# A routed attention and an FP4 feed-forward block on one core: weights decoded by pairs of units, the first LayerNorm folded, three gate/up banks, a staggered start

## The chip, the cores and the metric

The kernel runs on one core of a Trainium2 chip. The metric is the device time of one execution in microseconds (us). Engines: TensorE (PE; its weight loads are PEld), VectorE (DVE), ScalarE (ACT), GpSimd (POOL) and SyncE (SP), whose queue issues most DMAs. Each engine executes its own instructions in order and waits on semaphores for the others.

## The reference, cut to what matters

```
x = x + tanh(g_xattn) * attention(layernorm(x), ctx, router, W_q, b_q, token_sets)
x = x + tanh(g_ffn)   * ffn(layernorm(x), gate, up, down)     # weights: FP4 codes and block scales

attention: scores = ((x W_q^T + b_q) router^T) / sqrt(256), masked to a token's 4 drawn sets;
           softmax over the 2 largest, times ctx (64 sets x 256) of that sequence
ffn:       gate = x Wg^T, up = x Wu^T, out = (gelu_tanh(gate) * up) Wd^T, hidden size 2048
dequant:   two 4-bit codes in each int32 (low nibble first), a table of 16 values, one scale per 32 columns
```

x is 8 sequences of 256 tokens of 256 float32. LayerNorm has no weights: (x - mean) / sqrt(var + 1e-5).

## The kernel before, in words

**Feed-forward.** The hidden size is cut into 16 units of 128, the tokens into 4 chunks of 512 (two sequences each). One step s is one unit of one chunk: gate and up are projected (`project`, L909), ScalarE squares (L477), halves (L481) and takes tanh (L485), VectorE makes the cubic (L701), gate times up (L710) and the product (L717), ScalarE rounds it (`act_hi`, L493), GpSimd makes the rest (`act_lo`, L371), and `down` (L926) adds it into `acc_ps` two steps later. Every product is made in three parts (high x high, high x low, low x high), so gate, up and down are 6 matmuls of 128x512 each, 18 in a step.

**Decoding.** It happens once, inside chunk 0. For each unit `compact` (ScalarE, L411) takes the low bytes of the packed words, `unpack` (VectorE, L672 to L685, three stages) makes the bits of an 8-bit float, `scale_unit` (GpSimd, L352, two instructions of 384) multiplies by the scales, `turn_unit` (TensorE, L896) transposes six 128x128 blocks, `unit_high` (ScalarE, L419) and `unit_low` (VectorE, L693) store the two parts. Units 0 and 1 are turned into banks of the gate and up rings ahead of the loop, units 2 to 15 into `misc_ps` at the end of steps 0 to 13.

**Attention.** Sequences 0 and 1 are done ahead of the loop, the two of chunk c+1 during chunk c: each has 11 stages, one a step, which begin in steps 0 and 4 of the chunk. LayerNorm is: statistics (L568, L574, L579), the power -0.5 on GpSimd (`root`, L362), the shift (`center`, L586), and `normalise` on ScalarE (L437); it is done twice for each sequence. Scores, transposed probabilities, the attention product and the turned outputs all lie in `misc_ps`, as the turned units do. So TensorE waits (`unit_copied`) for the last unit's copies ahead of an attention stage of chunk 0, and for the attention stage's reader ahead of the next unit's turn.

The order on each engine is written out by hand. PSUM is full: two gate banks, two up banks, two of `acc_ps`, two of `misc_ps`.

## Time and profile before

| | us |
|---|---|
| three runs | 351.85, 348.82, 350.62 |
| median | 350.62 |
| profiled execution, first to last instruction (span) | 346.8 |
| TensorE busy in the span | 320.0 (92%) |
| VectorE, ScalarE, GpSimd busy | 232.1, 195.5, 132.8 |

The profiled execution has only its span on record; what lies around it is not in the profile, and the median of the three runs is 3.8 us above the span. The mean granted TensorE clock is 0.995 of full speed. Landmarks of the span: the first feed-forward product starts at 30.25, the gate of unit 2 at 40.36, the first gate of chunk 1 at 125.73, the last feed-forward product ends at 341.2.

### The profile page before, as it was taken

To read this page: it belongs to the slowest core of one execution; us is meant where nothing else is said; L and a number is where in the kernel's file an instruction comes from. 1 tells how busy PE (TensorE), PEld (TensorE's weight loads), DVE (VectorE), ACT (ScalarE), POOL (GpSimd) and SP (SyncE) were. 2 spreads that over 40 slices of the span, in tenths; PEclk is the share of its full clock that TensorE was granted. 3 is DMA by queue.
4 is the path that set the end of the run, shared out by engine and by line. 5 is a ranking of instruction groups with operands and counts; after the bars stand their busy time and mean duration, and the time that the engine had idled before them with its cause. 6 is when DMAs were issued, how large, how long until landed. Compare 5 with 4: busy or idle time off the path is not lost.

```text
span 346.8 us, 4565 instructions
## 1 busy us (share of the span) xinstructions
PE 320.0 (92%) x1482; PEld 261.2 (75%) x1482; DVE 232.1 (67%) x544; ACT 195.5 (56%) x379; POOL 132.8 (38%) x123
## 2 busy tenths in 40 slices
PE   2877979699779899999999999999999999999994
PEld 2846768488558788888878888888788888888882
DVE  3684799879888765685765565858675555555553
ACT  2624786655665757563646566664636575555551
POOL 4222475654646524251424342432343222333331
PEclk9999999989999999999999999999999999999999
DMA  6881101101000000000000000000000000000002
GB/s 150 139 211 47 45 5 43 46 12 35 2 0 0 3 1 0 2 0 0 2 1 30 2 31 0 2 0 1 2 0 30 30 4 0 0 2 0 30 0 92
DMA packets 22807, 8.68 MB, mean 25 GB/s; under 512 B 13760, under 2 KB 22784, under 8 KB 22784
## 3 DMA queue, kind: packets, MB, share of 16 engines
q1 hardware_dynamic: 22400, 8.07, 9.4%
q10 hardware_dynamic: 352, 0.33, 0.3%
q8 instruction: 11, 0.18, 0.2%
q14 instruction: 12, 0.10, 0.1%
q0 software_dynamic: 32, 0.00, 0.0%
HBM read 6.30 MB, written 2.10 MB: 24 GB/s over the span
## 4 chain that ended last, share of the span: by engine, by line
PE 72%; issue 13%; POOL 7%; DVE 4%; DMA 1%; ACT 1%; POOLq 0%; DVEq 0%
PE acc_ps L926 22%; PE gate_ps L909 21%; PE up_ps L909 21%; POOL w_nat L352 5%; PE misc_ps L884 2%; POOL act_lo L371 2%; PE misc_ps L858 1%; DMA tok_sb<-in_itok_Sx_dram 1%; PE misc_ps L867 1%; PE misc_ps L896 1%; POOL rstd L362 1%; PE misc_ps L939 1%; DVE act L701 1%; ACT normed L437 1%; DVE half_gu L710 0%
## 5 line engine op out<-in xcount | busy, mean ns | idle before, releaser
L371 POOL TENSOR_TENSOR act_lo<-act,act_hi 128x512 fp32r<-128x512 f32 x64 | 86.2, 1348 | 158.6 <-ACT act_hi L493 158.5
L701 DVE SCALAR_TENSOR_TENSOR act<-act,half_gu 128x512 f32<-128x512 f32 x64 | 46.3, 723 | 74.5 <-ACT half_gu L481 74.5
L477 ACT ACTIVATE act<-gate_ps 128x512 f32<-128x512 f32 x64 | 38.3, 598 | 90.2 <-PE gate_ps L909 90.2
L909 PE MATMUL gate_ps<-xt_hi,w_hi 128*128 128x512 f32 (+1 forms) x130 | 52.5, 404 | 0.6 <-DVE xt_lo L655 0.6
L717 DVE SCALAR_TENSOR_TENSOR act<-act,half_gu 128x512 f32<-128x512 f32 x64 | 48.3, 755 | 7.0 <-ACT act L485 5.1
L909 PE MATMUL gate_ps<-xt_lo,w_hi 128*128 128x512 f32 (+1 forms) x130 | 50.9, 392 | 0.0
L909 PE MATMUL gate_ps<-xt_hi,w_lo 128*128 128x512 f32 (+1 forms) x130 | 50.8, 391 | 0.0
L909 PE MATMUL up_ps<-xt_hi,w_lo 128*128 128x512 f32 (+1 forms) x130 | 50.8, 391 | 0.0
L909 PE MATMUL up_ps<-xt_hi,w_hi 128*128 128x512 f32 (+1 forms) x130 | 50.7, 390 | 0.0
L909 PE MATMUL up_ps<-xt_lo,w_hi 128*128 128x512 f32 (+1 forms) x130 | 50.7, 390 | 0.0
L485 ACT ACTIVATE act<-act 128x512 f32<-128x512 f32 x64 | 40.3, 630 | 12.8 <-DVE act L701 12.2
L710 DVE TENSOR_TENSOR half_gu<-up_ps,half_gu 128x512 f32<-128x512 f32 x64 | 44.0, 687 | 4.0
L352 POOL TENSOR_TENSOR w_nat<-code_bits,scales_sb 128x384 f32<-128x384 fp8e5 x32 | 31.3, 998 | 37.2 <-DVE code_bits L685 35.2
L926 PE MATMUL acc_ps<-act_hi,w_hi 128*128 128x512 f32 x128 | 42.1, 410 | 0.0
L493 ACT ACTIVATE act_hi<-act 128x512 fp32r<-128x512 f32 x64 | 40.6, 634 | 1.1 <-DVE act L717 1.1
L926 PE MATMUL acc_ps<-act_lo,w_hi 128*128 128x512 f32 x128 | 40.1, 395 | 0.2 <-POOL act_lo L371 0.2
L926 PE MATMUL acc_ps<-act_hi,w_lo 128*128 128x512 f32 x128 | 40.0, 394 | 0.0
L481 ACT ACTIVATE half_gu<-gate_ps 128x512 f32<-128x512 f32 x64 | 38.0, 594 | 0.0
L909 PEld LDWEIGHTS gate_ps<-xt_hi,w_hi 128*128 128x128 f32 x130 | 25.1, 193 | 5.5 <-issue 1.0
L909 PEld LDWEIGHTS gate_ps<-xt_hi,w_lo 128*128 128x128 f32 x130 | 25.1, 193 | 5.2
L909 PEld LDWEIGHTS up_ps<-xt_lo,w_hi 128*128 128x128 f32 x130 | 25.0, 192 | 5.0
L909 PEld LDWEIGHTS up_ps<-xt_hi,w_lo 128*128 128x128 f32 x130 | 25.0, 192 | 5.0
(85 smaller groups left out, 420.3 us busy)
## 6 DMA issues: line engine op xcount, KB each, us to landing
out_dram<-x_sb SPq DMA_DIRECT2D x8, 256.0 KB, 2.1
x_sb<-in_x_dram SPq DMA_DIRECT2D x1, 1536.0 KB, 8.2
packed<-L_ffn_gate_W_packed_dram SPq DMA_DIRECT2D x8, 128.0 KB, 2.2
packed<-n_L_ffn_up_W_packed_dram SPq DMA_DIRECT2D x8, 128.0 KB, 2.3
packed<-L_ffn_down_W_packed_dram SPq DMA_DIRECT2D x16, 64.0 KB, 2.1
x_sb<-in_x_dram SPq DMA_DIRECT2D x2, 256.0 KB, 3.2
ctx_sb<-in_ctx_dram SPq DMA_DIRECT2D x1, 384.0 KB, 9.5
half_gu<-in_L_xattn_W_q_dram ACTq DMA_DIRECT2D x1, 256.0 KB, 4.3
```

Source lines behind the costliest of these rows:

```text
L352: pool.tensor_tensor(w[:, :, i], codes[:, :, i], s, ALU.mult).then_inc(scaled, 1)
L371: pool.tensor_tensor(act_lo[:, s % 2, :], act[:, s % RING, :], act_hi[:, s % RING, :].bitcast(F32), ALU.subtract).then_inc(inter_lo, 1)
L477: sc.activation(act[:, s % RING, :], gate_ps[:, s % 2, :], ACT.Square)
L481: sc.activation(half_gu[:, s % 2, :], gate_ps[:, s % 2, :], ACT.Copy, scale=0.5).then_inc(halved, 1)
L485: sc.activation(act[:, s % RING, :], act[:, s % RING, :], ACT.Tanh, scale=2.0 * GELU_SCALE * GELU_CUBIC).then_inc(tanh_done, 1)
L493: sc.activation(act_hi[:, s % RING, :], act[:, s % RING, :], ACT.Copy).then_inc(inter_hi, 1)
L701: dve.scalar_tensor_tensor(a, a, 1.0 / GELU_CUBIC, half_gu[:, s % 2, :], ALU.add, ALU.mult).then_inc(cubic_done, 1)
L710: dve.tensor_tensor(h, up_ps[:, s % 2, :], h, ALU.mult).then_inc(gated_up, 1)
L717: dve.scalar_tensor_tensor(a, a, 1.0, half_gu[:, s % 2, :], ALU.add, ALU.mult).then_inc(inter_done, 1)
L884: i = pe.matmul(misc_ps[:, b % CB, h * D:(h + 1) * D], probs_t[:, b % CB, h * P:(h + 1) * P], ctx_sb[:, b, :], start=True, stop=True)
L909: i = pe.matmul(into[:, tok], wt[:, n, w], xt[:, c, k, tok], start=first, stop=(k, j) == last)
L926: i = pe.matmul(acc_ps[:, a, :], wt[:, n, 2 * D + a * P:2 * D + (a + 1) * P], h, start=(n == 0 and part == 0), stop=(n == UNITS - 1 and pa ...
```

## The change

1. **Pairs.** A pair r is units 2r and 2r+1, held in "rows of two" (`(r p v) j`), so each partition has 768 codes. There is one compact, one unpack (3 stages) and three scale instructions of 512 (`scale_rows_of` twice, `scale_down_of`) for a pair; one bank `dec_ps` takes the turned blocks as three tiles of four blocks each (gate and up of either unit, then the down blocks of both), and each tile has one copy on ScalarE (`tile_high`) and one on VectorE (`tile_low`), of 512 columns. A DMA group holds two pairs.
2. **First LayerNorm.** VectorE takes its row mean out of W_q (a reduce, a multiply, two adds); x itself is transposed (`turn_x`) and scored; the scores are multiplied by the root while they are read (`read_scores`, two instructions in place of one). `normalise` of the second LayerNorm goes from ScalarE to VectorE as one subtract-and-multiply for each half; `center` is gone.
3. **Banks.** Gate and up share three banks: the gate of step s waits for the gate-times-up of s-2, the up of step s for the halving of s-1. TensorE's order in a step is gate(s), up(s), down(s-2). `att_ps` (two banks) is left to attention and outputs.
4. **Start.** Sequence 0 and sequence 1 are staggered; the first token half of gate 0, up 0 and gate 1 is projected on sequence 0, the second half when sequence 1 is ready. So gate 1 is made ahead of the loop.
5. **Attention stages.** Nine in place of eleven; in chunk 0 they begin in steps 2 and 6, later in 0 and 4. Picking, weighing and spreading are ahead of the cubic on VectorE.
6. **Loads.** tokens by SyncE's queue in place of GpSimd's; W_q ahead of the router; x rows in pieces of 2 KB; all scales at once; `xt_hi` and `xt_lo` keep two chunks in place of four.

The order of the three parts of a product changes (`w_hi xt_hi`, `w_lo xt_hi`, `w_hi xt_lo`); their number does not. The core of the diff:

```diff
 TensorE, ahead of the loop
+            turn_router()
+            turn_x(0)
+            fold_router()
+            turn_x(1)
+            fold_bias()
+            score(0)
+            turn_probs(0)
+            attend(0)
+            score(1)
+            turn_tile(0)
+            turn_probs(1)
+            attend(1)
+            turn_tile(1)
+            turn_normed(0)
+            first_half, second_half = slice(0, ST), slice(ST, TOK)
+            pe.wait_ge(lo_stored, 1)
+            pe.wait_ge(xt_lo_ready, 1)
+            project(0, 0, 0, gu_ps[:, 0, :], first_half)
+            turn_normed(1)
+            project(0, 0, 1, gu_ps[:, 1, :], first_half)
+            pe.wait_ge(lo_stored, 2)
+            project(0, 1, 0, gu_ps[:, 2, :], first_half)
+            turn_tile(2)
+            pe.wait_ge(xt_lo_ready, 2)
+            project(0, 0, 0, gu_ps[:, 0, :], second_half).then_inc(gate_done, 1)
+            project(0, 0, 1, gu_ps[:, 1, :], second_half).then_inc(up_done, 1)
+            project(0, 1, 0, gu_ps[:, 2, :], second_half).then_inc(gate_done, 1)
 TensorE, a step
+                    if s >= 2:
+                        gate(s)
+                    if c == 0 and tile_after_gate(n) is not None:   # n odd
+                        turn_tile(tile_after_gate(n))
+                    if s >= 1:
+                        up(s)
+                    if c == 0 and tile_after_up(n) is not None:     # n even
+                        turn_tile(tile_after_up(n))
+                    if s >= LAG:
+                        down(s - LAG)
+                    ...  # turn_x, score, turn_probs, attend, turn_normed of the stage
+                    if c == 0 and tile_after_down(n) is not None:   # n odd
+                        turn_tile(tile_after_down(n))
+            def turn_tile(k):
+                r, t = divmod(k, 3)
+                pe.wait_ge(scaled, 3 * r + (2 if t < 2 else 3))
+                if k > 0:
+                    pe.wait_ge(lo_stored, k)
 ScalarE, ahead of the loop, from compact(0)
+            compact(0)
+            x_t_out(1)
+            lead_out(0)
+            compact(1)
+            probs_out(0)
+            lead_out(1)
+            probs_out(1)
+            tile_high(0)
+            ln2_high(0)
+            tile_high(1)
+            ln2_high(1)
+            tile_high(2)
+            compact(2)
 VectorE, ahead of the loop, from spread(0)
+            spread(0)
+            for stage in range(3):
+                unpack(0, stage)
+            input_variance(1)
+            add_attention(0)
+            update_stats(0)
+            update_variance(0)
+            read_scores(1)
+            find_top(1)
+            find_lead(1)
+            normalise(0)
+            find_where(1)
+            weigh(1)
+            spread(1)
+            tile_low(0)
+            ln2_low(0)
+            unpack(1, 0)
+            add_attention(1)
+            update_stats(1)
+            update_variance(1)
+            unpack(1, 1)
+            tile_low(1)
+            unpack(1, 2)
+            normalise(1)
+            ln2_low(1)
+            tile_low(2)
 VectorE, a step (stages of a sequence first)
+                    if c == 0 and n > 0 and tile_after_down(n - 1) is not None:
+                        tile_low(tile_after_down(n - 1))
+                    ...  # ln2_low; add, stats, variance; normalise; input_stats; pick; weigh and spread
+                    if c == 0 and n % 2 == 0 and n // 2 + 2 < PAIRS:
+                        for stage in range(3):
+                            unpack(n // 2 + 2, stage)
                     cubic(s)
+                    if c == 0 and tile_after_gate(n) is not None:
+                        tile_low(tile_after_gate(n))
                     gate_up(s)
                     combine(s)
+                    if c == 0 and tile_after_up(n) is not None:
+                        tile_low(tile_after_up(n))
 GpSimd, a step: low_part(s - 1), the roots, then
+                    if c == 0 and n % 2 == 1 and (n + 3) // 2 < PAIRS:
+                        for i in range(2):
+                            scale_rows_of((n + 3) // 2, i)
+                    if c == 0 and n % 2 == 0 and n // 2 + 1 < PAIRS:
+                        scale_down_of(n // 2 + 1)
```

In a step of chunk 0 ScalarE copies the down tile ahead of `square`, the tile after a gate behind it, and the tile after an up behind `tanh`; `compact` of a later pair follows `tanh` in odd steps.

## Rows read from the trace of the kernel before

**Rows 1.** Windows by stage: start:end, length, busy of each engine (count), granted clock, DMA.

```profile
30.00:40.36 10.36, 9.81 (x48) 9.04 (x49) 5.21 (x17) 5.59 (x12) 2.77 (x4) 1.00 0.15 40
40.36:125.73 85.37, 74.98 (x372) 60.52 (x370) 73.64 (x173) 53.37 (x109) 46.34 (x42) 0.98 0.07 19
125.73:341.23 215.50, 215.30 (x989) 176.62 (x987) 132.65 (x273) 123.93 (x232) 73.02 (x58) 1.00 0.02 8
```

**Rows 2.** Waits between 40.36 and 125.73: total us, times, longest.

```profile
DVE shift L586 <- POOL rstd L362: 5.0, 4, 1.2
...
PE misc_ps L858 <- issue: 5.4, 3, 2.8
...
PE misc_ps L874 <- DVE w_lo L693: 2.8, 1, 2.8
...
PE misc_ps L896 <- DVE xt_lo L655: 1.9, 1, 1.9
```

**Rows 3.** Timeline, TensorE: the turn after the split first step, and a plain step.

```profile
35.51 1.20 PE L896 MATMUL misc_ps<-ident,w_nat 128*128 128x128 f32 x6
...
84.50 0.81 PE L896 MATMUL misc_ps<-ident,w_nat 128*128 128x128 f32 x6
85.07 0.48 PE L909 MATMUL gate_ps<-xt_hi,w_hi 128*128 128x512 f32 x1
...
89.27 0.82 PE L896 MATMUL misc_ps<-ident,w_nat 128*128 128x128 f32 x6
```

**Rows 4.** The chain that ended last: start, us, what; six products without a wait.

```profile
121.81 1.36 PE gate_ps L909 x6
```

**Rows 5.** Timeline of the first 31 us: start, length, engine, line, tiles.

```profile
13.38 0.29 DVE L592 SCALAR_TENSOR_TENSOR scores<-misc_ps,score_bias 128x128 f32<-128x128 f32 x1 [0.48 <-PE misc_ps L867]
...
14.75 0.21 DVE L613 FIND_INDEX8 top_at<-top,scores 128x8 uint32<-128x64 f32 x1
14.84 1.49 PE L896 MATMUL gate_ps<-ident,w_nat 128*128 128x128 f32 x6
...
17.41 0.28 DVE L642 TENSOR_TENSOR probs<-probs_a,probs_b 128x128 f32<-128x128 f32 x1
...
19.34 0.20 DVE L672 TENSOR_SCALAR nibbles<-code_bytes 128x96 int32<-128x96 int32 x1
...
20.05 3.78 PE L884 MATMUL misc_ps<-ctx_sb,probs_t 64*128 64x256 f32 x8
20.09 0.26 DVE L685 TENSOR_SCALAR code_bits<-nibbles 128x192 int32<-128x192 int32 x1
...
22.16 0.69 DVE L650 TENSOR_TENSOR x_sb<-misc_ps,x_sb 128x512 f32<-128x512 f32 x1 [0.88 <-PE misc_ps L884]
...
29.68 0.60 ACT L460 ACTIVATE xt_hi<-misc_ps 128x512 fp32r<-128x512 f32 x1 [0.30 <-PE misc_ps L858]
...
30.25 0.55 PE L909 MATMUL gate_ps<-xt_hi,w_hi 128*128 128x256 f32 x1 [0.61 <-DVE xt_lo L655]
```

**Rows 6.** Groups by line and shape: busy us, mean ns, idle before.

```profile
L352 POOL TENSOR_TENSOR w_nat<-code_bits,scales_sb 128x384 f32<-128x384 fp8e5 x32 | 31.3, 998 | 37.2 <-DVE code_bits L685 35.2 <-issue 2.0
...
L362 POOL TENSOR_TENSOR rstd<-var_eps,minus_half 128x2 f32<-128x2 f32 x16 | 12.7, 792 | 7.1 <-DVE var_eps L579 6.6
...
L568 DVE BATCH_NORM_STATS2 stats<-x_sb 128x6 f32<-128x256 f32 x32 | 11.9, 412 | 3.8 <-DMA x_sb<-in_x_dram 3.8
...
L411 ACT ACTIVATE code_bytes<-packed 128x384 uint8<-128x384 uint8 x16 | 8.4, 526 | 0.0
```

**Rows 7.** Timeline, VectorE beside GpSimd in chunk 1.

```profile
146.80 1.29 POOL L371 TENSOR_TENSOR act_lo<-act,act_hi 128x512 fp32r<-128x512 f32 x1 [3.80 <-ACT act_hi L493]
...
146.91 1.20 DVE L619 CAST top_at<-top_at 128x4 f32<-128x4 uint32 x1
...
149.69 0.30 DVE L634 TENSOR_SCALAR probs_a<-iota_f,top_at,w_first 128x64 f32<-128x64 f32 x1
...
149.91 0.30 DVE L636 TENSOR_SCALAR probs_b<-iota_f,top_at,w_second 128x64 f32<-128x64 f32 x1
```

More of the change, by code:

```diff
@@ L286, in load_scales @@
[L286 to L296 removed]
+                sp.dma_start(x_sb[:, b0:b1, :], x_v[:, b0:b1, :]).then_inc(done, 16)
@@ L648, in add_attention @@
+                after(("first", b, HALVES - 1))
+                dve.tensor_tensor(probs[:, q, :, :], first[:, q, :, :], second[:, q, :, :], ALU.add).then_inc(probs_ready, 1)
             def add_attention(b):
+                q = b % CB
                 dve.wait_ge(attended, b + 1)
-                dve.tensor_tensor(tiles(b), misc_ps[:, b % CB, :], tiles(b), ALU.add).then_inc(x_updated, 1)
+                mark(("x_updated", b), dve.tensor_tensor(x_sb[:, b, :], att_ps[:, q, :], x_sb[:, b, :], ALU.add))
@@ new lines, in update_stats, with update_variance @@
+            def update_stats(b):
+                q = b % CB
+                after(("x_updated", b))
+                for h in range(HALVES):
+                    mark(("stats_2", b, h), dve.bn_stats(stats_2[:, q, h, :], half(b, h)))
+            def update_variance(b):
+                q = b % CB
+                for h in range(HALVES):
+                    after(("stats_2", b, h))
+                    mark(("moments_2", b, h), dve.bn_aggr(moments_2[:, q, h, :], stats_2[:, q, h, :]))
+                after(("moments_2", b, HALVES - 1))
+                dve.tensor_scalar(var_2[:, q, :], moments_2[:, q, :, 1], LN_EPS, None, ALU.add).then_inc(var_2_ready, 1)
@@ new lines, in normalise @@
+            def normalise(b):
+                q = b % CB
+                dve.wait_ge(rstd_2_ready, b + 1)
+                if b >= CB:
+                    dve.wait_ge(ln2_turned, b - CB + 1)
+                for h in range(HALVES):
+                    dve.tensor_scalar(normed[:, q, h, :].rearrange("p (i j) -> p i j", i=2),
+                                      half(b, h).rearrange("p (j i) -> p i j", i=2),
+                                      moments_2[:, q, h, 0:1], rstd_2[:, q, h:h + 1],
+                                      ALU.subtract, ALU.mult).then_inc(normed_ready, 1)
@@ L791, in _ @@
                     s = c * UNITS + n
-                    ahead = n + DECODE_LEAD if c == 0 and n + DECODE_LEAD < UNITS else None
-                    def attention(*parts):
-                        for stage, part, *ln in parts:
-                            for b in next_sequences(c, n, stage):
-                                part(b, *ln)
-                    if c == 0 and LEAD <= n + 1 < UNITS:
-                        unit_low(n + 1)
-                    attention((CENTER_1, center, 0), (CENTER_2, center, 1), (STATS_1, tile_stats, 0),
-                              (STATS_2, tile_stats, 1), (WEIGH, find_where), (SPREAD, spread))
@@ L804, in _ @@
-                    if ahead:
-                        unpack(ahead, 0)
+                    if c == 0 and n > 0 and tile_after_down(n - 1) is not None:
+                        tile_low(tile_after_down(n - 1))
+                    for b in next_sequences(c, n, SPLIT_LO):
+                        ln2_low(b)
+                    for b in next_sequences(c, n, ADD):
+                        add_attention(b)
+                        update_stats(b)
+                        update_variance(b)
+                    for b in next_sequences(c, n, CENTER):
+                        normalise(b)
@@ L1009, in _ @@
+                    if c == 0 and tile_after_up(n) is not None:
+                        turn_tile(tile_after_up(n))
                     if s >= LAG:
                         down(s - LAG)
[L1012 to L1018 removed]
+                    for b in next_sequences(c, n, STATS_1):
+                        turn_x(b)
@@ new lines, in _ @@
+                    for b in next_sequences(c, n, SCORE):
+                        score(b)
+                    for b in next_sequences(c, n, WEIGH):
+                        turn_probs(b)
+                    for b in next_sequences(c, n, ATTEND):
+                        attend(b)
+                    for b in next_sequences(c, n, CENTER):
+                        turn_normed(b)
+                    if c == 0 and tile_after_down(n) is not None:
+                        turn_tile(tile_after_down(n))
@@ L1019, in _ @@
+                    if c > 0 and n in AT_OUT:
+                        turn_output((c - 1) * CB + AT_OUT.index(n))
+            for s in range(STEPS - LAG, STEPS):
                 down(s)
```

793 lines of the change are left out of this document (365 added, 428 removed).

## The prediction

> **What bounds the kernel now.** I cut the span at landmarks of TensorE's timeline and read the windows first. From the first gate of chunk 1 (125.73) to the last product (341.23) TensorE is busy 215.30 of 215.50 us [rows 1]. No room for a wait on another engine is left there, so only fewer or faster products would shorten it. From the gate of unit 2 (40.36) to 125.73 it is busy 74.98 of 85.37 us: 10.4 us idle, while VectorE is busy 73.64. The waits of that window name the places [rows 2]: TensorE stands ahead of attention's transposes in `misc_ps` (5.4 us in 3 waits, 2.8, 1.9), where it wants the last unit's copies. They are late in steps where VectorE has attention work; one cause of that is `center`, which waits 5.0 us in four times for a root that stands behind `act_lo` on GpSimd. Ahead of 40.36 lie chains of short instructions. So there are three terms: the time to unit 2's gate, the 14 steps behind it, the 215.5 us.
>
> **What doesn't change.** Six products take 1.36 us [rows 4], a step 18 products, 4.08 us, before and after. "No zero products" takes none out: the diff keeps three parts for gate, up and down, 96 transposed weight blocks, four fp32 score products a sequence. The new order of the parts costs nothing, as each loads its own weights either way. The tail keeps its work.
>
> **Term 1, to unit 2's gate.** Before, the steps are done for both sequences together; after, nearly one by one, on engines that keep their order. I walk the orders with the starts and lengths of the rows [rows 5, 6].
> Scores of sequence 0: `normalise` and its shift fall out, but W_q (256 KB) must land (I take 5.1 to 5.8, where its first user starts now) and be centred, four VectorE instructions, some 1.2 us. `fold_router`, `turn_x(1)`, `fold_bias` and `score(0)` follow on TensorE: the scores are read at 12.3 against 13.38. Read to search took 13.38 to 14.96, 1.6 us [rows 5]; with weights, four comparisons 0.22 apart [rows 7] and an addition some 3.3 us, so `probs(0)` at 15.7 against 17.69 (17.41 + 0.28).
> `attend` for two sequences takes 3.78, and the first addition starts 2.1 behind the start [rows 5]: attention 0 added from 18.9 against 22.16. Then addition 0.6, statistics 0.65 to 0.8 (two of 0.41) and variance 0.45 [rows 5, 6]: 20.6. Now VectorE does sequence 1's scores, `normalise(0)` (two instructions of 256; no row shows them, so half of the 0.69 for 512 each, 0.6 when they follow without a gap; bounds 0.4 and, behind a GpSimd instruction, 1.8) and the 3.3 us chain: `probs(1)` at 24.3.
> TensorE's queue holds `turn_normed(0)` behind `turn_probs(1)`, `attend(1)` and `turn_tile(1)`. From 24.3: turn 0.65, copy 0.4, attend 1.9, then four transposes of 0.25 (six took 1.49 [rows 5]) twice: 29.2. Two copies of 0.6: the first half product at 30.6, against 30.25, and on one sequence.
> Sequence 1's addition stands on VectorE behind `ln2_low(0)`, 30.5. From there: unpack stage 0.3, addition 0.6, statistics and variance 1.1, unpack 0.55, `tile_low(1)` 0.6, unpack 0.35, normalise 0.3 for its first half: 34.4. TensorE has idled since 31.9. Transposes 0.9; then half products. Before, 24 of them took 30.25 to 35.51 [rows 3, 5], 0.22 each: twelve are 2.6; `turn_tile(2)` 0.9: 38.8.
> From its end: copy 0.6, `compact(2)` 0.8 (0.53 for 384, most of it by the byte [rows 6]), unpack 1.5 (a unit took 1.0, 19.34 to 20.35 [rows 5]; two are between that and 2.0), cubic, tanh, copy, low copy 2.6: 44.4. Turn 0.5; square, halve, copy and low copy of tile 4 1.4; turn 0.5: unit 2's gate at 46.7. By the same cut that is 40.36 before: **+6.3 us**. The bounds: +2.5, if TensorE's transposes and half products go at full pace (0.1 and 0.12 each, as 0.57 for six in chunk 0 [rows 3] and half of 0.227), to +9, if the first group of weights, now 768 KB in place of 384, holds `compact(0)` and the lead behind it by 2.7 us.
>
> **Term 2, the 14 steps.** Before: 14 x 4.08 = 57.1 us; two steps with a turn are 4.77 apart [rows 3], so 12 turns cost 0.69 each, 8.3. Attention's price on TensorE comes from the stage without a wait: 215.5 less 48 steps and the 2 lagging downs, 198.6, is 16.9 for 4 sequences and 6 turned outputs; at 0.57 an output, 3.4 a sequence, 6.8 for the two in chunk 0. Then idle 10.4; the rest of 85.37, 2.8 us, is small gaps and 2% of granted clock [rows 1]. After: the same 57.1 and 6.8; 18 tiles of four blocks at 0.49 (6 blocks 0.57 plus 0.12 behind) 8.8; gaps 0.9, as no wait above 1.5 us is left that the clock fell behind. That is 73.6 with no wait.
> Waits that remain: a tile can turn only when both copies of the last are made. In an even step VectorE does the low copy, stage work X, unpack 1.5, cubic, gate times up, combine and the next low copy: 5.3 us + X from the step's start, where TensorE wants the tile at 5.9 + its own attention work. In odd steps X up to 1.8 is free. With X = 1.1 (input statistics), 0.95 (picking), 2.2 (weighing), 1.7 (addition), 0.6 (normalise, split) the steps 2, 4, 5, 8 and 9 wait 0.5 to 1.4, the other nine nothing: 4.1 us. GpSimd's three instructions of 512 (1.0 for 384 in the loop, so 1.3 [rows 6]) give 3.9 in two steps, less than its 4.0 before. Sum 77.7: **-7.7 us**, with -12 for no waits and -2 for double.
>
> **Term 3, the rest.** Spreading and `turn_probs` now stand in one step: the probabilities are ready 2.1 us into VectorE's step, TensorE wants them at 2.7. If the last instruction meets `act_lo` on GpSimd it waits 1.2, as the cast did at 146.91 [rows 7]: 0 to 0.7 for each of four sequences. I take **+0.7 us**; the bounds are 0 and +3. ScalarE loses 4 x 0.6 us a sequence, worth nothing beside an idle-free TensorE. The three banks cost nothing: the gate of s waits for a gate-times-up that ended 4 us earlier, the up of s for a halving that has 2.7 us. The cover is VectorE's 1.8 us of work in 4.08; it would have to fall 3 us behind.
>
> **Sum.** 6.3 - 7.7 + 0.7 = -0.7 us. The profiled span would be 346.1, and with the same 3.8 around it the median 349.9.
>
> **The port.** A VectorE cast of 128x4 took 1.20 us, more than a 128x64 comparison's 0.30, while GpSimd's `act_lo` ran, and ended with it [rows 7]. The Trainium skill (SBUF — State Buffer, "Who interferes with whom") says that a VectorE operation in a two-port mode and a GpSimd operation share one port pair, and that "the other fully blocks" for the whole instruction; the trace agrees. By that page longer GpSimd instructions speak against this change, as each blocks for longer; it is a rival below.
>
> **Rivals.**
> *A, the walk is too slow.* TensorE goes at full pace ahead of 40 us and chunk 0 has nearly no waits. For it: turns in the loop go 0.1 a block. Against: blocks took 0.25 ahead of 30 us. Term 1 +2.5, term 2 -9: 350.6 - 6.5 = 344.1.
> *B, VectorE and GpSimd block each other.* Two scale instructions stand behind `act_lo` without a gap, 3.9 us, and reach into the even step where VectorE unpacks. VectorE was busy 73.64 of 85.37 already; what must precede a turn is on its queue. If each of six even steps loses a further 1.0 and each weighing 0.7, it is slower: 349.9 + 6 = 355.9. It decides as soon as the low copy ends later than 5.9 us into the step. Against: the tile chain has 0.6 us of slack, and the four blocked `center`s are gone.
> *C, the first group of weights is late.* Then +2.7 on term 1: 352.6. Against: `compact(0)` ran unhindered at 11.2, and the new packets are larger.
> *D, the order ahead of the loop does nothing it should,* or the gain and loss cancel elsewhere: 350.6.
>
> **How the numbers follow.** Forecast 0.40, its own range 347 to 353; A 0.28, B 0.17, C 0.08, D 0.07. Three runs of before lie 3 us apart, so 1%, 3.5 us, is about what a measurement can tell from no change. Faster (below 347.1): A, and a fifth of the forecast, 0.36. Slower (above 354.1): B, half of C and a little of the forecast, 0.23. Same: 0.41. The range takes in A and the near part of B: 342.5 to 356.
>
> **What would show it.** Right: first half product near 30.6, a TensorE hole of about 2.5 us behind it that ends with `normalise(1)`; unit 2's gate near 46.7; first gate of chunk 1 near 124.7; no hole there above 1.5; 216 us from there to the last product. Wrong: the first product ahead of 28 (the scores' chain mis-sized), a gate of unit 2 ahead of 43 (A), holes in every even step of chunk 0 with unpack or cubic over 1.2 us (B), or holes behind `turn_probs` in chunks 1 and 2.

## The result, and the profile after

The changed kernel takes 357.44 us (median of 4 runs, 356.88 to 357.82), the kernel before 350.57 in the runs beside it (348.82 to 351.85): ratio 1.0203, interval 1.0157 to 1.0249. Forecast were 349.9 and a range of 342.5 to 356. The profiled spans are 356.0 and 346.8 us, 9.2 apart.

The spans differ by more than the medians. The profiled execution of the changed kernel took 357.82 us around a span of 356.0, 1.8 more, and wherever both are on record the time is 1.8 to 3.0 us over the span. So the 3.8 us that the prediction put around the span is too much: the profile before comes from an execution some 2 us under the kernel's median (the run of 348.82 fits). The terms below, cut from the two profiles, therefore add up to 9.2, where the medians differ by 6.9.

Cut at the same landmarks as [rows 1], that is unit 2's gate, the first gate of chunk 1 and the last product, the windows of the changed kernel are (start:end, length, busy time of TensorE, its weight loads, VectorE, ScalarE, GpSimd, granted clock, DMA):

```profile
50.73:134.28 83.55, 77.23 (x370) 61.97 (x369) 72.01 (x144) 46.78 (x87) 42.57 (x37) 0.95 0.08 23
134.28:350.40 216.12, 215.59 (x989) 176.21 (x987) 140.37 (x276) 116.23 (x215) 73.11 (x58) 1.00 0.02 8
```

| term | before | forecast | after |
|---|---|---|---|
| 1: to unit 2's gate | 40.36 | +6.3 | 50.73, +10.4 |
| 2: the 14 steps | 85.37 | -7.7 | 83.55, -1.8 |
| 3: to the last product | 215.50 | +0.7 | 216.12, +0.6 |

So the time was lost at the start, and the steps that should have paid for it gave back a quarter of what I had counted on.

**The start.** The timeline of the changed kernel at the places where my walk and the chip part:

```profile
9.68 0.20 ACT L474 ACTIVATE gates<-gates_in 128x2 f32<-128x2 f32 x1 [0.67 <-DMA gates_in<-in_g_ffn_dram]
9.71 0.40 POOL L361 COPY half_gu<-bq_sb 128x256 f32<-128x256 f32 x1 [8.25 <-DMA gates_in<-in_g_ffn_dram]
...
13.09 0.47 DVE L553 SCALAR_TENSOR_TENSOR scores<-att_ps,rstd,score_bias 128x64 f32<-128x64 f32 x2 [0.49 <-PE att_ps L846]
...
19.87 0.69 DVE L599 TENSOR_TENSOR x_sb<-att_ps,x_sb 128x512 f32<-128x512 f32 x1 [1.57 <-PE att_ps L863]
...
22.50 1.05 POOL L350 TENSOR_TENSOR w_nat<-code_bits,scales_sb 128x512 f32<-128x512 fp8e5 x1
22.67 0.90 DVE L567 TENSOR_TENSOR lead<-top 128x2 f32<-128x2 f32 x1
...
23.49 0.73 DVE L622 TENSOR_SCALAR normed<-x_sb,moments,rstd 128x256 f32<-128x256 f32 x2
...
26.49 0.64 PE L853 MATMUL att_ps<-ident,probs 128*64 128x128 f32 x2 [3.90 <-DVE probs L594]
...
33.06 0.55 PE L895 MATMUL gu_ps<-xt_hi,w_hi 128*128 128x256 f32 x1 [1.50 <-DVE xt_lo L630]
...
36.30 1.47 DVE L622 TENSOR_SCALAR normed<-x_sb,moments,rstd 128x256 f32<-128x256 f32 x2
```

The reader is to see small slips that add up: the scores are read 0.8 late, the addition comes 1.0 late, a 128x2 subtraction takes 0.90 us beside a GpSimd scale (0.16 for sequence 0, at 13.99), and so `probs(1)` is ready at 26.43 against the forecast 24.3, and TensorE has nothing to do for 3.90 us ahead of `turn_probs(1)`. The first half product is at 33.06 against 30.6. Behind it sequence 1's `normalise` takes 1.47 us, also beside a scale, where sequence 0's took 0.73, and unit 2's gate is at 50.73 against 46.7.

**The steps.** The waits of TensorE in 50.73 to 134.28, then VectorE and GpSimd ahead of the longest but one of them, in the timeline:

```profile
PEld dec_ps L887 <- issue: 8.3, 5, 3.0
PE dec_ps L887 <- DVE w_lo L663: 6.2, 3, 2.6
```

```profile
67.08 1.32 POOL L357 TENSOR_TENSOR act_lo<-act,act_hi 128x512 fp32r<-128x512 f32 x1 [2.15 <-ACT act_hi L464]
67.28 1.34 DVE L656 TENSOR_SCALAR code_bits<-nibbles 128x384 int32<-128x384 int32 x1
...
68.36 1.17 POOL L350 TENSOR_TENSOR w_nat<-code_bits,scales_sb 128x512 f32<-128x512 fp8e5 x1
...
68.54 1.54 DVE L675 SCALAR_TENSOR_TENSOR act<-act,half_gu 128x512 f32<-128x512 f32 x1
...
72.43 0.72 PE L887 MATMUL dec_ps<-ident,w_nat 128*128 128x128 f32 x4 [2.49 <-DVE w_lo L663]
...
73.38 0.63 PE L895 MATMUL gu_ps<-xt_hi,w_lo 128*128 128x512 f32 x1
...
73.80 0.63 PE L895 MATMUL gu_ps<-xt_lo,w_hi 128*128 128x512 f32 x1
```

All of TensorE's waits there (1.17, 2.49 and 2.56 us) are for a tile's low copy: those of the even steps 2, 4 and 8, three of the five that the prediction named, which TensorE wants in the odd step behind each. VectorE's two instructions end 0.2 and 0.55 us behind the GpSimd instruction beside each: 1.34 us for what takes 0.36 alone, 1.54 for 0.68. And after this wait the products follow 0.42 us apart and not 0.23: the clock is at the lower of its two levels. The granted clock is 0.83 on the mean of 70-80 and of 100-110, behind the two long waits, and 0.88 in 50-60, behind one of 3.03 us that ends at 47.68, ahead of these steps.

**The rest.** In 134.28 to 350.40 TensorE has two waits, 0.3 and 0.2 us, none of them behind `turn_probs`, and the tail is as before.

### The profile page after: what moved, and what is told of

It is laid out like the page before. It is cut to its first block, busy times and chain, and to the rows that moved or that the text cites. A ratio compares the mean times of both kernels' runs of the same rounds, so it can differ in the third digit from the quotient of the medians.

```text
span 356.0 us, 4453 instructions
## 1 busy us (share of the span) xinstructions
PE 323.2 (91%) x1488; PEld 262.5 (74%) x1488; DVE 243.3 (68%) x515; ACT 178.5 (50%) x331; POOL 128.6 (36%) x115
## 4 chain that ended last, share of the span: by engine, by line
PE 78%; DVE 14%; issue 5%; ACT 1%; POOL 1%; POOLq 0%; DVEq 0%
PE gu_ps L895 44%; PE acc_ps L930 22%; PE att_ps L863 3%; PE dec_ps L887 3%; PE att_ps L846 2%; DVE act L675 2%; DVE act L688 2%; DVE half_gu L682 1%; DVE code_bits L656 1%; PE att_ps L872 1%; DVE nibbles L650 1%; DVE w_lo L663 1%; PE att_ps L945 1%; DVE normed L622 1%; PE att_ps L836 1%
## 5 line engine op out<-in xcount | busy, mean ns | idle before, releaser
L895 PE MATMUL gu_ps<-xt_hi,w_hi 128*128 128x512 f32 (+1 forms) x262 | 107.6, 411 | 1.5 <-DVE xt_lo L630 1.5
L895 PE MATMUL gu_ps<-xt_lo,w_hi 128*128 128x512 f32 (+1 forms) x262 | 103.4, 394 | 0.0
L895 PE MATMUL gu_ps<-xt_hi,w_lo 128*128 128x512 f32 (+1 forms) x262 | 103.1, 394 | 0.0
L450 ACT ACTIVATE act<-gu_ps 128x512 f32<-128x512 f32 x64 | 38.3, 598 | 96.2 <-PE gu_ps L895 96.0
L895 PEld LDWEIGHTS gu_ps<-xt_hi,w_hi 128*128 128x128 f32 x262 | 50.9, 194 | 12.4 <-issue 3.5
L895 PEld LDWEIGHTS gu_ps<-xt_lo,w_hi 128*128 128x128 f32 x262 | 50.9, 194 | 10.7
L895 PEld LDWEIGHTS gu_ps<-xt_hi,w_lo 128*128 128x128 f32 x262 | 51.1, 195 | 8.7
L682 DVE TENSOR_TENSOR half_gu<-gu_ps,half_gu 128x512 f32<-128x512 f32 x64 | 44.2, 691 | 6.6 <-PE gu_ps L895 0.6
L453 ACT ACTIVATE half_gu<-gu_ps 128x512 f32<-128x512 f32 x64 | 38.0, 593 | 0.0
L930 PEld LDWEIGHTS acc_ps<-act_hi,w_lo 128*128 128x128 f32 x128 | 24.5, 191 | 5.3
```

The lines of the kernel that those rows point to most:

```text
L450: sc.activation(act[:, s % RING, :], gu_ps[:, 2 * s % GU_RING, :], ACT.Square)
L453: sc.activation(half_gu[:, s % RING, :], gu_ps[:, 2 * s % GU_RING, :], ACT.Copy, scale=0.5).then_inc(halved, 1)
L682: dve.tensor_tensor(h, gu_ps[:, (2 * s + 1) % GU_RING, :], h, ALU.mult).then_inc(gated_up, 1)
L895: i = pe.matmul(into[:, tok], wt[:, n, w], xt[:, c % 2, k, tok], start=first, stop=(k, j) == last)
L930: i = pe.matmul(acc_ps[:, a, :], wt[:, n, GU + a * P:GU + (a + 1) * P], h, start=(n == 0 and part == 0), stop=(n == UNITS - 1 and part == 2))
```

## The experiments

Gate 2 is the start of unit 2's gate, the 14 steps run from there to the first gate of chunk 1, busy is TensorE's busy time and clock its granted mean in them. The ratio is to the kernel before, run beside it (350.6 us beside the changed kernel, 348.9 to 349.1 beside the others). The changed kernel was not run again beside them, so a difference of a microsecond to its 357.4 says nothing.

The times of a row are medians, and its first four figures come from one profiled execution, which need not be a middle one: that of e3 took 354.3 us, 2.1 over its median, those of e7, e10 and e15 1.3 to 1.7 under theirs. A difference of 2 us between two of the windows can be that alone.

| run | gate 2 | 14 steps | busy, clock | us | ratio, interval |
|---|---|---|---|---|---|
| changed | 50.73 | 83.55 | 77.23, 0.95 | 357.4 | 1.020, 1.016-1.025 |
| e1 short low | 51.02 | 76.80 | 73.23, 1.00 | 351.0 | 1.006, 1.004-1.008 |
| e2 unpack late | 50.39 | 85.80 | 77.65, 0.94 | 359.0 | 1.027, 1.020-1.034 |
| e3 lockstep | 44.88 | 86.56 | 75.22, 0.98 | 352.3 | 1.009, 1.005-1.012 |
| e4 sequence 1 first | 50.13 | 82.62 | 76.27, 0.96 | 356.3 | 1.021, 1.015-1.027 |
| e5 tile early | 49.04 | 86.53 | 77.27, 0.96 | 359.3 | 1.030, 1.023-1.036 |
| e6 e3 and e5 | 44.67 | 86.16 | 75.50, 0.98 | 353.0 | 1.011, 1.003-1.018 |
| e7 e6, work split | 43.53 | 79.97 | 75.18, 0.97 | 347.6 | 0.996, 0.993-1.000 |
| e8 down first | 50.39 | 83.37 | 75.52, 0.98 | 357.7 | 1.026, 1.019-1.033 |
| e9 e7, weights late | 44.92 | 79.08 | 75.12, 0.98 | 349.1 | 0.998, 0.994-1.001 |
| e10 e9, loads early | 44.59 | 77.61 | 73.79, 0.99 | 349.2 | 0.999, 0.996-1.002 |
| e11 before, short low | 40.37 | 75.94 | 73.01, 1.00 | 339.9 | 0.971, 0.967-0.975 |
| e12 loads early | 50.68 | 83.86 | 73.92, 1.00 | 358.1 | 1.024, 1.020-1.028 |
| e13 low in halves | 51.06 | 82.33 | 75.41, 0.98 | 356.9 | 1.020, 1.016-1.025 |
| e14 before, halves | 40.33 | 82.40 | 74.54, 0.98 | 345.7 | 0.988, 0.984-0.993 |
| e15 e7, halves | 43.84 | 79.93 | 75.01, 0.97 | 348.5 | 0.996, 0.993-0.999 |
| e16 e7, short low | 44.50 | 73.99 | 72.94, 1.00 | 341.5 | 0.976, 0.972-0.980 |

**e1, a short low part.** In chunk 0 `act_lo` covers 32 columns:

```
-                pool.tensor_tensor(act_lo[:, s % RING, :], act[:, s % RING, :],
+                w = 32 if s < UNITS else TOK
+                pool.tensor_tensor(act_lo[:, s % RING, 0:w], act[:, s % RING, 0:w],
...
```

> The changed kernel, but in chunk 0 GpSimd makes act_lo over 32 columns of 512 in place of all (the buffers are cleared once at the start), so the low third of chunk 0's down products is nearly all left out; nothing else moves, TensorE does every product. Port theory (the two holes of 2.5 us, at 69.9 and 96.8, come from VectorE and GpSimd blocking each other around unpack and the cubic): the 64-element instructions of 1.3 us fall to about 0.2, unpack's last stage falls from 1.34 to 0.36 us, both holes shrink below 1 us, the clock doesn't fall behind them: the window from unit 2's gate to chunk 1 falls from 83.5 to 76 to 79 us, the time by 4 to 8 us to about 351. Rival (VectorE's queue is too long in those steps whatever GpSimd does): the holes stay above 2 us and the time within 2 us of 357.4.

6.4 us went, and 6.75 of the 14 steps. The two holes shrank to 1.50 and 1.58 us, not below 1, and TensorE is idle for 3.6 us in all. It looked like the whole answer; e11 below shows that it isn't.

**e2, unpack behind the combination** in even steps:

```
-                    (ahead of cubic)  for stage in range(3): unpack(n // 2 + 2, stage)
+                    (behind combine and tile_low)  the same
```

> The changed kernel with the three unpack stages of an even step of chunk 0 moved from ahead of the cubic to behind combine and the low copy of the tile. No work is left out. Chain theory (unpack stands on the way from one tile's low copy to the next, so its 1.5 us and what blocks it end in TensorE's holes): the holes at the second turn of steps 2, 4 and 8 (1.2, 2.5, 2.6 us) vanish, with them two or three falls of the clock: chunk 0's window 83.5 to 75 to 78, the time about 350. Rival (VectorE's total load decides, not the order): the work only moves to the next step, holes come up at the other turns or behind weighing, and the time stays within 2 us.

TensorE still waits three times ahead of a turn, but for 2.5 us in all where it was 6.2, and two other holes came ahead of `turn_probs` (2.79 us at 73.6, 2.50 at 102.4). Moving the load moves the hole.

**e3, both sequences together ahead of the loop**, each stage for 0 and then for 1, as in the kernel before; on VectorE:

```
             spread(1)
             tile_low(0)
-            ln2_low(0)
             unpack(1, 0)
+            unpack(1, 1)
+            add_attention(0)
+            update_stats(0)
+            update_variance(0)
             add_attention(1)
...
```

> The changed kernel with sequences 0 and 1 done together ahead of the loop, as before: on each engine a stage of sequence 0 is followed by the same stage of sequence 1; gate 0 and up 0 are still made in halves, gate 1 whole. No work is left out. Theory of the stagger (7 to 10 us are lost ahead of unit 2's gate since each sequence passes the short chains alone, and sequence 1 waits behind sequence 0's split): unit 2's gate comes at 43 to 46 in place of 50.7, the time falls by 5 to 7 us. Rival (that start is late because of the pair's longer decode and the one bank for turned blocks): unit 2's gate stays behind 49 and the time within 2 us.

Gate 2 comes 5.85 us sooner: more than half of term 1 is the stagger. The median falls by 5.2. The 14 steps are 3.0 longer in the profiled execution, which was the slowest of 11, so how much of that belongs to the edit is open; that the decoding enters them with less of a lead is my reading, and no run tests it.

**e4, sequence 1's addition ahead of `ln2_low(0)`** (and both its unpack stages):

> The changed kernel with one change in VectorE's order ahead of the loop: two unpack stages, the attention's addition and the statistics of sequence 1 ahead of sequence 0's ln2_low, for which VectorE idled 3.5 us (28.7 to 32.2). No work is left out. Theory (sequence 1 is late by its place in VectorE's queue): normalise(1) starts at about 34 in place of 36.3, TensorE's 2.1 us hole behind the first half product goes, unit 2's gate and the time come 2 us earlier. Rival (the chain of the copies and turns behind it sets the gate of unit 2): under 0.7 us.

The hole ahead of `turn_normed(1)` went from 2.08 to 0.79 us, but gate 2 moved by 0.6 only. That one tie of the start is not where its time lies.

**e5, the tile's copies ahead of tanh and combine**, and **e6**, the same with e3:

```
-                    combine(s)
                     if c == 0 and tile_after_up(n) is not None:
                         tile_low(tile_after_up(n))
+                    combine(s)
```

> The changed kernel; the tile turned behind an up is copied sooner: on ScalarE ahead of tanh in place of behind it, on VectorE ahead of combine in place of behind it. No work is left out. Chain theory (what holds TensorE is the low copy, which stands behind cubic, tanh and combine in even steps): the wait for tanh and combine, 1.2 to 1.4 us, leaves the chain: the holes ahead of the second turn of a pair (3.0 ahead of the loop, then 1.2, 2.5, 2.6) lose 1 to 1.4 us each, two falls of the clock go with them, the time falls by 5 to 8 us to about 350. Rival (VectorE's sum of work decides): the wait shows up in the next tile and the time falls by less than 2 us.

> Both the lock-step start and the earlier copies of the tile behind an up. No work is left out. If the two causes (stagger, tile chain) are separate, their gains add up: the first took 5.2 us, the second is expected at 5 to 8, so 344 to 347, faster than the kernel before. If they share one resource (VectorE's work in chunk 0), the earlier start is given back in the loop as the lock-step kernel did in part (its 14 steps took 86.6 us for 83.6), and the time stays at 350 to 352.

Both missed: e5 is no faster than the changed kernel, and e6 is where e3 is. Let the tiles be earlier and the weighing lands on GpSimd's instructions instead. The timeline of e5:

```profile
70.74 2.41 DVE L591 TENSOR_SCALAR first<-iota_f,top_at,w_first 128x64 f32<-128x64 f32 x2
70.80 1.29 POOL L357 TENSOR_TENSOR act_lo<-act,act_hi 128x512 fp32r<-128x512 f32 x1 [3.95 <-ACT act_hi L464]
```

Two comparisons that take 0.53 us together elsewhere took 2.41, beside `act_lo` and the scale that follows it at 72.05.

**e7, e6 with VectorE's work spread over the steps**: the index search goes to the picking step, the unpack stages behind the combination and the third to the next step, `turn_probs` a step later.

```
+                    if c == 0 and n % 2 == 1 and n // 2 + 2 < PAIRS:
+                        unpack(n // 2 + 2, 2)
                     if c == 0 and tile_after_up(n) is not None:
                         tile_low(tile_after_up(n))
                     combine(s)
+                    for b in next_sequences(c, n, PICK):
+                        find_where(b)
+                    if c == 0 and n % 2 == 0 and n // 2 + 2 < PAIRS:
+                        for stage in range(2):
+                            unpack(n // 2 + 2, stage)
```

> The kernel with the lock-step start and the earlier copies, and VectorE's work of a step spread: find_where goes to the picking step behind combine; two unpack stages behind combine in even steps, the third behind gate-times-up in odd steps; TensorE turns the probabilities a step later, behind the gate. No work is left out. Queue theory: with no more than 1.5 us of stage work ahead of any cubic no hole above 1 us is left in chunk 0, the 14 steps take 75 to 78 us and the time is 340 to 344. Rival (VectorE with GpSimd's blocks is full in chunk 0): holes stay at the turns, the 14 steps take over 81 us, the time over 346.

9.8 us under the changed kernel and the first not slower than the kernel before. The medians of e7 and e6 differ by 5.4 us, and the 14 steps by 6.2 in two executions that flatter e7 (1.3 under its median, 0.7 over that of e6). Two holes are left, 2.26 and 2.47 us, in the steps that weigh, and the time is above the 344 of the queue theory.

**e8, GpSimd scales the down rows ahead of `act_lo`** in even steps:

> The changed kernel with one change of GpSimd's order: in even steps of chunk 0 the scaling of the down blocks goes ahead of act_lo of the last unit. No work is left out. Port theory: at 67 to 70 us unpack's last stage was held by act_lo and the cubic behind it by the down scaling, one straight after the other; with the scaling done earlier, while VectorE waits for ScalarE, the cubic's 1.54 us at 68.54 falls to 0.7, the holes of 2.5 us lose 0.8 to 1 us each, the time falls by 2 to 5 us. Rival (GpSimd's order doesn't matter, its total does, or act_lo now comes late for down): within 1 us, or slower.

The cubic of 1.54 us took 0.68 as it should, and the hole behind it fell from 2.49 to 1.62. But the next cubic, beside the next `act_lo`, took 1.78, and TensorE waited in more places (1.40 us at 58.7, 0.90 at 75.4, 0.45 at 84.2, 2.24 at 97.5), 7.8 us in all where it was 6.2: no gain.

**e9, e7 with the weights behind the tile's low copy**, and **e10**, e9 with the bias and gates loaded early:

```
-                    for b in next_sequences(c, n, WEIGH): ...   (ahead of cubic)
                     cubic(s)
...
                         tile_low(tile_after_up(n))
+                    for b in next_sequences(c, n, WEIGH): ...
                     combine(s)
```

> The kernel that split the picks and started both sequences together has two holes left over 2 us in its turning stretch, both in the step that weighs (2.26 us at 66.47 and 2.47 us at 91.81, each waiting for the down tile's low copy), with a granted clock of 0.83 in 90-100. Here the weights and the spread stand behind the tile's low copy and the product of gate and up, directly ahead of the combination. Theory (VectorE's order in the steps that hold a sequence's work, with waits for GpSimd's instructions on top, is what the 14 steps lose): both holes fall under 0.8 us, the clock stays at 1.00 from 50 us on, and the stretch from unit 2's gate to chunk 1's first gate goes from 80.0 to 76-77 us; median 343-345.5 us. Rival (the total on VectorE is what counts, and work put elsewhere makes another hole): a hole over 1.5 us turns up in the combination's or the next cubic's place, the stretch stays over 79 us, and the median is within 1 us of 347.6.

> The kernel with the weights late, and in addition the loads of the query bias and the two gates stand directly behind the first sequence's in SyncE's queue, ahead of the codes of the gate rows. In the changed kernel the gates landed at 9.68 us and held up the bias column, and so the first scores (read at 13.09). Theory (the start is a chain in which the bias column is late by 0.8 us): the bias and the gates land by 7 us, the first scores are read 0.5-1.0 us sooner, and unit 2's gate and the end come 0.5-1.0 us sooner than without this edit. Rival (the codes behind them land later, and the decoding of the first tile becomes the start's end): unit 2's gate does not come sooner, or up to 1 us later.

The rival of e9 is nearer. The holes didn't go, they changed place: the waits of TensorE in e9, 40 to 120 us:

```profile
PE att_ps L856 <- DVE probs L594: 3.9, 2, 2.0
PE dec_ps L890 <- DVE w_lo L663: 2.7, 2, 2.0
```

The medians are 349.1 and 349.2 us against e7's 347.6, so neither edit is worth anything that these runs can show.

**e11, the kernel before with the short low part**: the control that e1 lacked.

> The kernel before, with GpSimd's low part of the activation in chunk 0 over 32 of 512 columns (the other columns of that part stay zero, so most of that part's product is left out; the products themselves are as many). The same edit took 6.4 us from the changed kernel. Theory A (the kernel before paid for the same waits: its cubic takes 852 ns on the mean where 0.68 us is its time alone, and its two index copies 1,092 ns): it gains 1-3 us, less than the changed one, because its largest holes (2.80 at 69.14 and 2.78 at 95.61) stand behind other waits; median 346-348.5. Rival (what GpSimd's low part costs is the same in both kernels and says nothing on the change): it gains 5.5-7 us, median 342-343.5.

Both theories missed, on the far side: 9.0 us, the 14 steps from 85.37 to 75.94. The kernel before lost more to GpSimd's low part (9.4 us) than the changed one (6.7).

Where it lost them is in VectorE's busy time, which fell from 73.64 to 62.86 us for the same 173 instructions. The largest part is `center`, four instructions of 128x2. The groups of the 14 steps, in the kernel before and in e11:

```profile
L586 DVE SCALAR_TENSOR_TENSOR shift<-mean_var,rstd 128x2 f32<-128x2 f32 x4 | 4.9, 1233 | 5.0 <-POOL rstd L362 5.0
```

```profile
L588 DVE SCALAR_TENSOR_TENSOR shift<-mean_var,rstd 128x2 f32<-128x2 f32 x4 | 0.7, 170 | 4.4 <-POOL rstd L363 4.4
```

The wait for the root hardly moved (5.0 to 4.4 us), since the root stands behind the scaling of a unit and not behind `act_lo`. It is `act_lo` that stands behind the root, and beside it each `center` took 1.23 us for 0.17: 4.2 us, and the changed kernel has no `center`. The windows of the 14 steps, e11 and then e1:

```profile
40.37:116.31 75.94, 73.01 (x372) 59.47 (x370) 62.86 (x173) 53.30 (x109) 30.83 (x42) 1.00 0.08 21
```

```profile
51.02:127.82 76.80, 73.23 (x370) 59.16 (x369) 65.11 (x144) 46.64 (x87) 27.05 (x35) 1.00 0.08 25
```

With that wait out of both, the steps are nearly as long in one kernel as in the other, TensorE has the same 73 us of work in them, and VectorE is busy 2.2 us longer in the changed one, in fewer instructions. GpSimd's scaling still runs in both: the cubic and the combination take 818 and 861 ns on the mean in e1, 693 and 772 in e11. ScalarE has 6.7 us less to do, but 4.4 of that is `normalise`, which the change drops or gives to VectorE. No run has the decoding by pairs alone, so what it is worth is not shown; the whole change relieves neither TensorE nor VectorE in these steps.

**e12, the bias and gates loaded early** in the changed kernel, directly behind the first sequence's load:

> The changed kernel with only this edit: the loads of the query bias and of the two gates stand directly behind the first sequence's in SyncE's queue. The prediction put the first scores' reading at 12.3 us, and it came at 13.09 since the bias column waits for these loads until 9.7. Theory (those 0.8 us go down the chain of the start): scores are read at 12.2-12.6, the first half product starts 0.5-0.8 us before 33.06, and the median is 0.3-1.0 us under 357.4. Rival (the chain of the start has a later tie, the transfers or sequence 1's rows): first half product within 0.2 us of 33.06, no change in the median.

The theory failed, and the rival's "no change in the median" is nearer (358.1): the loads only changed places. The bias was there at 6.96 and the gates by 8.1, but the tokens' comparison then waited to 9.27 (6.50 in the changed kernel) and TensorE for sequence 1's rows to 9.93 (8.49). The scores were read at 13.60, 0.5 later and not sooner, and the first half product came at 33.56 for 33.06:

```profile
9.27 0.69 DVE L702 TENSOR_TENSOR act<-tok_sb,iota_i 128x512 f32<-128x512 int32 x1 [2.80 <-DMA tok_sb<-in_itok_Sx_dram]
...
9.93 1.11 PE L836 MATMUL att_ps<-ident,x_sb 128*128 128x128 f32 x4 [2.03 <-DMA x_sb<-in_x_dram]
```

This run says something on the clock as well. Its 14 steps took 83.86 us with TensorE busy 73.92 at a granted 1.00, those of the changed kernel 83.55 with 77.23 at 0.95. So in these two executions the time of the slower products is time that TensorE otherwise waited:

```profile
50.68:134.54 83.86, 73.92 (x372) 58.89 (x370) 72.44 (x144) 47.42 (x88) 44.29 (x37) 1.00 0.07 23
```

**e13 to e15, the low part in two halves** of 256 columns, in the changed kernel, in the one before and in e7:

```
+                parts = 2 if s < UNITS else 1
+                for i in range(parts):
+                    w = slice(i * TOK // parts, (i + 1) * TOK // parts)
+                    pool.tensor_tensor(act_lo[:, s % RING, w], act[:, s % RING, w], ...
+                                       ALU.subtract).then_inc(inter_lo, 2 // parts)
...
```

> The changed kernel with only this edit: GpSimd makes the low part of an activation in chunk 0 in two instructions of 256 columns each and not in one of 512 (some 1.3 us, its rows say). Theory (a VectorE instruction of the kinds that waited starts its work only when the GpSimd instruction under way has ended, so the wait is as long as what is left of it): the cubics that took 1.54 and 1.80 us take at most 1.3, the holes before the turns shrink from 2.5 to under 2, the 14 steps take 80-82.5 us against 83.55, and the median is 1-3.5 us under 357.4. Rival (the price goes by elements or by load, and two instructions cost more of the two engines' time than one): 83-86 us and a median within 1 us or above.

> The kernel before with the same edit, the low part in two halves. It lost 9.4 us of its 14 steps to the whole low part. Theory (waits for whole instructions): 82-84.5 us for the 14 steps against 85.37, and a median 1-3.5 us under that of the kernel before. Rival (by load): no gain, or a loss up to 2 us.

> The version with both sequences together at the start, tiles' copies early and the picks split (347.6, its 14 steps 80.0 us), with the low part in two halves. Theory: holes at 66.5 and 91.8 from 2.3-2.5 to under 2, clock at 1.00 from 50 us on, 77.5-79 us for the 14 steps, median 344.5-346.5, the fastest of all that compute everything. Rival: within 1 us of 347.6 or slower.

The same edit gives the kernel before 3.0 us of its 14 steps and 1.2% of its time, as the theory of e14 said. It gives the changed one 1.2 us of its steps, less than its median can show, and e7 nothing. In e13 the group of `code_bits` fell from 1092 to 696 ns on the mean, but the cubic stayed (1055, from 1030 in the changed kernel) and a half of the low part took 868 where half of 1332 is 666. Groups of e13, 50 to 120 us:

```profile
L360 POOL TENSOR_TENSOR act_lo<-act,act_hi 128x256 fp32r<-128x256 f32 x24 | 20.4, 868 | 36.9 <-ACT act_hi L468 36.9
...
L679 DVE SCALAR_TENSOR_TENSOR act<-act,half_gu 128x512 f32<-128x512 f32 x11 | 11.6, 1055 | 0.0
```

So neither theory covers all three runs: the wait isn't simply a matter of whole instructions, and isn't by elements either. e14 is the fastest kernel here that computes everything: 345.7 us, interval of the ratio 0.984 to 0.993.

**e16, e7 with the short low part**: how low the changed decoding can go.

> The same version (347.6) with the low part of chunk 0 over 32 of 512 columns; the other columns stay zero, so that most of that part is left out while the products are as many. It shows the floor of the changed decoding in an order that suits it. TensorE is busy 73.0 us in the 14 steps of the kernel before and 73.2 in those of the changed one where GpSimd's low part is short. Theory A (the change took no work from TensorE in these steps, and once VectorE is free the steps are TensorE's own): 73.5-75.5 us for the 14 steps, so at most 2 us less than the 75.94 of the kernel before with the same edit, and a median of 341-343, not below the 339.9 of that one, since the start is 3 us later. Rival (the new decoding has a floor well below): under 72 us, median under 339.5.

Theory A held, 73.99 us with TensorE busy 72.94. In an order that suits it the changed kernel's steps are 1.95 us shorter than those of the one before with the same edit, and its time isn't below that of e11, since gate 2 comes 4.1 us later.

## Why the prediction was wrong

**What bounds the kernel now**: right on the place. The 10.4 us of idle time were the only ones to be had, and VectorE's lateness was their cause: with the low part short (e11) 7.5 of them went, and 2.0 us of slower products with them. The reason that I gave for the lateness was misread. The root that `center` waits for stands behind the scaling, not behind `act_lo`, and these waits stayed (5.0 to 4.4 us) when the low part was short. What went was the time that `center` itself took beside `act_lo` (4.9 to 0.7 us), a cost that I had counted as VectorE's work.

**Term 1**, the step that failed second: +10.4 for +6.3, 4.0 us short and beyond its own bound of +9. That a stagger costs time was in the walk and is right (e3: doing one sequence after the other costs 5.85 us); the size is off. The walk priced each instruction from a row and put next to nothing between them. It lacked the wait for the gates' load (0.8), 0.17 in each of two `attend`s (2.07 for 1.9), and GpSimd instructions in the way of VectorE: 0.74 in the lead (0.90 for 0.16) and 0.9 in two `normalise` (1.47 for 0.6). That is some 2.8 of the 4.0, by my estimate from these rows. A further 0.9 lies in the last two turns: from the low copy's end at 47.53 to unit 2's gate took 3.2 us for 2.3, and the products there follow 0.42 us apart from 49.2 on. The rest lies in handovers too short to name. Removing a single tie helps little (e4 0.6 us, e12 none): the next is right behind. Rival C (late weights) didn't occur: `compact(0)` waited 0.54 us for them at 10.42 and did not hold the lead.

**Term 2**, the step that failed most: -1.8 for -7.7, 5.9 us short and just outside its bound of -2. The walk through the new order came out within 0.9 us: with the low part short the changed kernel's steps take 76.80 us (e1), TensorE idle for 3.6 of them, where I had 77.7 with 4.1 of waits. The 73.6 "with no wait" is close as well, to e16's 73.99. What failed is the price of the low part, which the sum puts at nothing: VectorE held up by GpSimd's instructions, 6.75 us in the changed kernel (83.55 less 76.80). I had it only in rival B, and the argument against B, "the four blocked `center`s are gone", is true and covers 4.2 us of the price before, not the 6.75 that came with the new order. In the 83.55 us TensorE was idle for 6.3, and its busy time was 4.0 over e1's at the lower clock. Both stand for one delay of VectorE's, as the comparison with e12 indicates.

What is more, I took the new order's own gain for granted. It has none: with the short low part the changed kernel's steps take 76.80 us and those of the one before 75.94. The term can be written by runs alone: 9.4 less 6.7 is 2.7 gained on GpSimd's low part, less 0.9 for the order, 1.8.

**Term 3**: +0.6 for +0.7, right in number and by luck. The wait that I priced, behind `turn_probs`, does not exist; there are 0.3 us more of waits elsewhere (0.3 ahead of `turn_x`) and 0.3 us more of busy time. **The banks cost nothing**: right, no wait names them. **The rule on the port**: I cited the Trainium skill (SBUF — State Buffer, "Who interferes with whom") as a rival at 355.9. A delay of the kind that it describes decided here, 0.6 to 1.1 us an instruction; but by my reading of the page the change should have come out worse on that count, and the runs show that the kernel before paid more for it. Whether each of VectorE's late instructions was in the mode that the page speaks of, no run shows.

**The chances.** 0.17 for B was too low, and its price was added up wrongly: six even steps at 1.0 and two weighings at 0.7 are 7.4, not 6, which gives 357.3. That this is nearly the 357.4 measured is chance, as term 1 and the 3.8 us around the span were off as well. The reasons for and against B were weighed without the rows that would have told: the group means of VectorE in the kernel before. The row of `center` (1,233 ns) stands under e11. By line, 50 to 125 us:

```profile
L701 DVE SCALAR_TENSOR_TENSOR act<-act,half_gu 128x512 f32<-128x512 f32 x13 | 11.1, 852 | 2.9 <-ACT half_gu L481 2.9
L717 DVE SCALAR_TENSOR_TENSOR act<-act,half_gu 128x512 f32<-128x512 f32 x12 | 9.4, 784 | 0.3 <-ACT act L485 0.3
```

Alone they take 0.68 (e16: 693 and 717 on the mean). This is VectorE busy only in name, and it was there to be read.

**Open** is what pairs, the folded LayerNorm, the banks and the loads do each by itself, as no run has one of them alone; why halves help the kernel before and not the changed one, and what of the start's remaining 4 us (44.5 to 44.9 in e3, e9, e10 and e16, where the kernel before has 40.36) belongs to which part; each of these is one profile, and e7's says 43.53.

## What to carry to other kernels

Where the mean time of an instruction lies above the time of the same instruction alone, a wait hides in busy time: compare the two before you count an engine's work as fixed. Whoever starts units earlier by doing sequences one after the other pays in the chain ahead of the loop, and a walk through a chain of short instructions needs an allowance for each handover. And a run that shortens a suspect is worth little without the same run on the kernel before: e1 alone would have blamed the change for a cost that both kernels have.

## What the runs showed of the hardware

- VectorE instructions beside a GpSimd tensor operation took two to seven times as long and ended with it or up to 0.6 us behind: a 128x512 product of sums 1.54 for 0.68 us, 128x384 shifts 1.34 for 0.36, 128x64 comparisons 1.2 each for 0.27, a 128x2 product 1.23 for 0.17. Products of 128x512 that read PSUM (`gate_up`, `tile_low`) stood at 0.68 to 0.69 on the mean in all runs.
- Behind the holes of 3.0, 2.5 and 2.6 us (ending at 47.7, 72.4 and 99.4) the granted clock fell, with 0.42 us a product for 0.23; behind the like hole of 2.5 us at 72.2 in e12 it didn't, and the steps took as long. In the kernel before it fell behind a hole of 2.80 us (0.68 in 69-73) and not behind one of 2.79 (1.00 in 95-98).
- Moving three small loads ahead of a large one (e12) delayed those behind by 1.4 to 2.8 us, and nothing was gained.
